# First scan: expert tiles handled in pairs, one tanh and two VectorE operations for both

## The reference, cut to what matters

```python
xn = layernorm(x)
# scan: h is kept for each of 256 features and 16 states
h = dA_t * h + dBx_t ;  y_t = einsum('bdn,bn->bd', h, C_t)
# experts: 176 inner rows
h = silu(x @ w_gate.T) * (x @ w_up.T) ;  acc = acc + h @ w_down.T * cw
x = x + scan(xn) + experts(xn)
```

## Time and profile before

| | |
|---|---|
| median of three runs | 1195.89 us (1195.59 to 1200.48) |
| profiled execution, its own time | 1205.48 us |
| its span, first to last instruction | 1203.7 us |
| busy TensorE, VectorE | 976.7, 914.1 us |
| busy ScalarE, GpSimd | 497.0, 434.9 us |
| mean granted TensorE clock | 0.935 |

### The profile page before, as it was taken

One profiled execution on the slowest core, in us unless ns is written; L12 is line 12 of the kernel. 1 busy time (PEld: TensorE's weight loads), 2 busy tenths in 40 slices (PEclk: granted clock), 3 DMA queues, 4 the chain that ended last, 5 costly groups with the idle time before them and its releaser, 6 DMA issues. The chain is left out here.

```text
span 1203.7 us, 18601 instructions
## 1 busy us (share of the span) xinstructions
PE 976.7 (81%) x6048; PEld 578.1 (48%) x6048; DVE 914.1 (76%) x1506; ACT 497.0 (41%) x1130; POOL 434.9 (36%) x332
## 2 busy tenths in 40 slices
PE   3987997788787778773787686889988988899885
PEld 2354555444444444441634353445555555456553
DVE  4659567989999999999657746677677767677676
ACT  2201135554555555543121124545455554554542
POOL 0000100777787877753171010322322232133310
PEclk9989999989999999995798798999998999999998
DMA  6960172787878878878650041443433343244524
GB/s 220 369 172 1 52 164 74 134 155 144 165 148 156 162 149 159 147 141 182 142 148 5 0 99 38 112 95 86 112 87 93 87 106 93 67 95 104 116 40 141
DMA packets 107092, 143.27 MB, mean 119 GB/s; under 512 B 30022, under 2 KB 97334, under 8 KB 102710
## 3 DMA queue, kind: packets, MB, share of 16 engines
q0 software_dynamic: 30368, 77.92, 33.5%
q1 hardware_dynamic: 76630, 64.14, 19.2%
HBM read 72.80 MB, written 39.46 MB: 93 GB/s over the span
## 5 line engine op out<-in xcount | busy, mean ns | idle before, releaser
L1501 POOL DMA_INDIRECT sum<-yo,to_i x48 | 78.0, 1624 | 317.1 <-ACT yo L1459 301.2
L1171 POOL DMA_INDIRECT xg<-xn_d,token_i x80 | 96.2, 1203 | 175.1 <-DVE to_i L460 93.4
L1164 POOL DMA_INDIRECT sum<-yo,to_i x80 | 140.3, 1754 | 46.8 <-DMA sum<-yo,to_i 23.7
L1011 PE MATMUL bank<-areaA,xgT 128*128 x320 | 120.6, 502 | 15.0 <-issue 9.9
L1028 PE MATMUL bank<-areaA,hidT 88*128 x320 | 91.7, 410 | 45.8 <-ACT hidT L1076 41.7
L2048 DVE TENSOR_TENSOR areaD<-areaD,gb 128x512 f32<-128x512 f32 x128 | 87.5, 688 | 53.0 <-ACT areaD L1995 49.2
L1028 PEld LDWEIGHTS bank<-areaA,hidT 88*128 88x128 f32 x320 | 55.6, 193 | 76.7 <-issue 72.1
L686 PE MATMUL bank<-xnT,areaB 128*128 128x512 f32 x192 | 86.8, 599 | 0.8 <-DVE y L716 0.8
L1846 PE MATMUL bank<-xnT,w_in 128*128 128x512 f32 x160 | 85.5, 661 | 2.2 <-ACT ecn L1751 1.5
L1011 PEld LDWEIGHTS bank<-areaA,xgT 128*128 128x128 f32 x320 | 56.8, 196 | 58.0 <-issue 41.5
L1491 POOL DMA_INDIRECT xg<-xn_d,token_i x48 | 53.9, 1123 | 82.6 <-DVE to_i L460 68.2
(11 more groups left out here) (342 smaller groups left out, 2141.6 us busy)
## 6 DMA issues: line engine op xcount, KB each, us to landing
y<-xnT POOLq DMA_DIRECT2D x21, 1024.0 KB
wst<-gu_f SPq DMA_DIRECT2D x96, 176.0 KB
y<-areaB POOLq DMA_DIRECT2D x11, 1024.0 KB
wst<-down_f SPq DMA_DIRECT2D x48, 176.0 KB
areaA<-in_gu SPq DMA_DIRECT2D x2, 2816.0 KB
gu_f<-in_gu POOLq DMA_DIRECT2D x1, 5632.0 KB, 17.0
sum<-yo SPq DMA_DIRECT2D x2, 2176.0 KB, 16.2
down_f<-in_down POOLq DMA_DIRECT2D x1, 2816.0 KB, 22.6
```

Source lines behind the costliest of these rows:

```text
L1011: last = nc.tensor.matmul(bank[:, GB + q % 2, 0:2 * FI], xgT[:, q % 2, k, :], wgu0_of(e, k), start=(k == 0), stop=(k == KD - 1))
L1164: nc.gpsimd.indirect_dma_start(sum0_d[q % 2], bass.IndirectOffsetOnAxis(ap=to_i[:, q:q + 1], axis=0), yo[:, q % 5, :], None, compute_op=AL ...
L1171: nc.gpsimd.indirect_dma_start(xg[:, q % 5, :], None, xn_d[0], bass.IndirectOffsetOnAxis(ap=token_i[:, q:q + 1], axis=0)).then_inc(s.gathe ...
L1501: nc.gpsimd.indirect_dma_start(sum1_d, bass.IndirectOffsetOnAxis(ap=to_i[:, q:q + 1], axis=0), yo[:, q % 4, :], None, compute_op=ALU.add). ...
```

## The change

Tiles go in pairs of six ticks. tile_at(t, ahead, at) gives the tile q = 2m + ahead whose step stands at place `at` of pair m's six ticks, which begin at tick 6m + 1. One tanh of 128 x 2 x 176 reads both banks when both gate products are there (gu_full at q + 2), and the two VectorE operations work on both tiles. On TensorE the order in pair m is: hidden transposes of 2m, x transposes of 2m+2, down of 2m, gate and up of 2m+2, x transposes of 2m+3, hidden transposes of 2m+1, gate and up of 2m+3, down of 2m+1. On ScalarE: hT_copy 2m, xT_copy 2m+2, y_copy 2m, xT_copy 2m+3, hT_copy 2m+1, the tanh of pair m+1, y_copy 2m+1, with the decays at their ticks as before. VectorE does pair m's operations at tick 6m + 1. Before the loop the first two tiles are transposed and multiplied. GpSimd's and SyncE's lists are unchanged.

```diff
+        UNIT, TILE, PAIR = 4, 3, 6
+        def tile_at(t, ahead, at):
+            m, step = divmod(t - 1, PAIR)
+            q = 2 * m + ahead
+            return q if step == at and 0 <= q < NT0 else None
 def hid_transposes(pe, q):
-            pe.wait_ge(s.hid_ready, q + 1)
+            pe.wait_ge(s.hid_ready, q // 2 + 1)
 def layer0_tensor(pe):
-            x_transposes(pe, 0)
-            gate_up(pe, 0)
-            x_transposes(pe, 1)
+            for q in range(2):
+                x_transposes(pe, q)
+                gate_up(pe, q)
...
+                for ahead, at in ((0, 0), (1, 3)):
+                    q = tile_at(t, ahead, at)
+                    if q is not None: hid_transposes(pe, q)
+                q = tile_at(t, 2, 0)
+                if q is not None: x_transposes(pe, q)
...
+                for ahead, at in ((2, 2), (3, 3)):
+                    q = tile_at(t, ahead, at)
+                    if q is not None: gate_up(pe, q)
+                q = tile_at(t, 3, 2)
+                if q is not None: x_transposes(pe, q)
+                for ahead, at in ((0, 1), (1, 4)):
+                    q = tile_at(t, ahead, at)
+                    if q is not None: down(pe, q)
 def gate_tanh(act, q):
-            act.wait_ge(s.gu_full, q + 1)
-            nc.scalar.activation(act_t[:, q % 2, :], bank[:, GB + q % 2, 0:FI], ACT.Tanh, scale=0.5)
+            act.wait_ge(s.gu_full, q + 2)
+            nc.scalar.activation(act_t[:, :, :], bank[:, GB:GB + 2, 0:FI], ACT.Tanh, scale=0.5)
 def layer0_scalar(act):
+            xT_copy(act, 1)
             gate_tanh(act, 0)
-            xT_copy(act, 1)
...
+                q = tile_at(t, 2, 4)
+                if q is not None: gate_tanh(act, q)
+                for ahead, at in ((0, 0), (1, 3)):
+                    q = tile_at(t, ahead, at)
+                    if q is not None: hT_copy(act, q)
+                for ahead, at in ((2, 0), (3, 2)):
+                    q = tile_at(t, ahead, at)
+                    if q is not None: xT_copy(act, q)
+                for ahead, at in ((0, 1), (1, 4)):
+                    q = tile_at(t, ahead, at)
+                    if q is not None: y_copy(act, q)
 def silu(v, q):
-            v.wait_ge(s.tanh_ready, q + 1)
+            v.wait_ge(s.tanh_ready, q // 2 + 1)
-            first = scalar_tensor_tensor(act_t[:, q % 2, :], act_t[:, q % 2, :], 1.0, bank[:, GB + q % 2, 0:FI], ...)
+            first = scalar_tensor_tensor(act_t[:, :, :], act_t[:, :, :], 1.0, bank[:, GB:GB + 2, 0:FI], ...)
-            scalar_tensor_tensor(hid[:, q % 2, :], act_t[:, q % 2, :], 0.5, bank[:, GB + q % 2, FI:2 * FI], ...)
+            scalar_tensor_tensor(hid[:, :, :], act_t[:, :, :], 0.5, bank[:, GB:GB + 2, FI:2 * FI], ...)
 def layer0_vector(v):
-                if t == 1:
-                    silu(v, 0)
-                if part == 2 and q + 1 < NT0:
-                    silu(v, q + 1)
+                q = tile_at(t, 0, 0)
+                if q is not None: silu(v, q)
```

More of the change, by code:

```diff
@@ L952, in phase0_vector @@
             v.wait_ge(vec.sem, vec.now)
-        UNIT, TILE = 4, 3
+        UNIT, TILE, PAIR = 4, 3, 6
         TICKS0 = UN * UNIT
-        assert TICKS0 >= TILE * (NT0 + 2)
+        assert NT0 % 2 == 0 and TICKS0 >= TILE * (NT0 + 2)
+        def tile_at(t, ahead, at):
+            m, step = divmod(t - 1, PAIR)
+            q = 2 * m + ahead
+            return q if step == at and 0 <= q < NT0 else None
         BROW, CROW, XB, HY, GB = 0, 2, 4, 5, 6
@@ L1032, in layer0_tensor @@
             pe.wait_ge(s.w_expert, 64)
-            x_transposes(pe, 0)
-            gate_up(pe, 0)
-            x_transposes(pe, 1)
+            for q in range(2):
+                x_transposes(pe, q)
+                gate_up(pe, q)
             for t in range(TICKS0):
-                q, part = divmod(t, TILE)
                 pair = (t + 1) // (2 * UNIT)
@@ L1040, in layer0_tensor @@
                     b_product(pe, pair)
[L1041 to L1044, removed]
+                for ahead, at in ((0, 0), (1, 3)):
+                    q = tile_at(t, ahead, at)
+                    if q is not None:
+                        hid_transposes(pe, q)
+                q = tile_at(t, 2, 0)
+                if q is not None:
+                    x_transposes(pe, q)
                 if t and t % (2 * UNIT) == 0:
                     c_product(pe, t // (2 * UNIT))
[L1047 to L1050, removed]
+                for ahead, at in ((2, 2), (3, 3)):
+                    q = tile_at(t, ahead, at)
+                    if q is not None:
+                        gate_up(pe, q)
+                q = tile_at(t, 3, 2)
+                if q is not None:
+                    x_transposes(pe, q)
+                for ahead, at in ((0, 1), (1, 4)):
+                    q = tile_at(t, ahead, at)
+                    if q is not None:
+                        down(pe, q)
         def decay(act, u):
@@ L1068, in gate_tanh @@
         def gate_tanh(act, q):
-            act.wait_ge(s.gu_full, q + 1)
-            nc.scalar.activation(act_t[:, q % 2, :], bank[:, GB + q % 2, 0:FI], ACT.Tanh, scale=0.5).then_inc(s.tanh_ready, 1)
+            act.wait_ge(s.gu_full, q + 2)
+            nc.scalar.activation(act_t[:, :, :], bank[:, GB:GB + 2, 0:FI], ACT.Tanh, scale=0.5).then_inc(s.tanh_ready, 1)
         def hT_copy(act, q):
@@ L1095, in layer0_scalar @@
             act.wait_ge(delta_ready, 4)
+            xT_copy(act, 1)
             gate_tanh(act, 0)
-            xT_copy(act, 1)
             for t in range(TICKS0):
[L1099 to L1107, removed]
+                q = tile_at(t, 2, 4)
+                if q is not None:
+                    gate_tanh(act, q)
+                for ahead, at in ((0, 0), (1, 3)):
+                    q = tile_at(t, ahead, at)
+                    if q is not None:
+                        hT_copy(act, q)
+                for ahead, at in ((2, 0), (3, 2)):
+                    q = tile_at(t, ahead, at)
+                    if q is not None:
+                        xT_copy(act, q)
+                for ahead, at in ((0, 1), (1, 4)):
+                    q = tile_at(t, ahead, at)
+                    if q is not None:
+                        y_copy(act, q)
                 if t % UNIT == 0 and t // UNIT + 1 < UN:
@@ L1111, in silu @@
         def silu(v, q):
-            v.wait_ge(s.tanh_ready, q + 1)
-            first = vec.done(nc.vector.scalar_tensor_tensor(act_t[:, q % 2, :], act_t[:, q % 2, :], 1.0, bank[:, GB + q % 2, 0:FI], ALU.add, ALU.mult))
+            v.wait_ge(s.tanh_ready, q // 2 + 1)
+            first = vec.done(nc.vector.scalar_tensor_tensor(act_t[:, :, :], act_t[:, :, :], 1.0, bank[:, GB:GB + 2, 0:FI], ALU.add, ALU.mult))
             v.wait_ge(vec.sem, first)
-            nc.vector.scalar_tensor_tensor(hid[:, q % 2, :], act_t[:, q % 2, :], 0.5, bank[:, GB + q % 2, FI:2 * FI],
+            nc.vector.scalar_tensor_tensor(hid[:, :, :], act_t[:, :, :], 0.5, bank[:, GB:GB + 2, FI:2 * FI],
                                            ALU.mult, ALU.mult).then_inc(s.hid_ready, 1)
@@ L1124, in layer0_vector @@
             for t in range(TICKS0):
-                if t == 1:
-                    silu(v, 0)
-                q, part = divmod(t, TILE)
-                if part == 2 and q + 1 < NT0:
-                    silu(v, q + 1)
+                q = tile_at(t, 0, 0)
+                if q is not None:
+                    silu(v, q)
                 u = t // UNIT
```

## The result

The changed kernel takes **1233.71 us**, the median of four runs (1231.38 to 1235.96); the kernel before took 1198.18 beside it (1195.59 to 1205.55). The ratio is **1.0255 [1.0215, 1.0295]**: slower, as forecast, but by about 30 us instead of 7.7 (the two medians lie 35.5 us apart; four executions of before that spread over 10 us don't settle which of the two it is). 1203.6 was predicted, and 1233.7 lies outside the range of 1185 to 1222.

What follows compares the result with a forecast made beforehand. VectorE, nearly full in the first scan stage, was taken to bound the kernel. Stage 346.9 + 20.1 + 4.6 + 3.0 = 374.6 us, 7.7 more than now, gave 1203.6 us; range 1185 to 1222.

Steps and rivals of the forecast that it cites:

- VectorE's own work: First scan with the experts beside it: 309.3 scan, 36.4 pair operations, 1.2 left over, 346.9 us without any wait.
- waits, odd pairs, at the tanh: VectorE before an odd pair's operations: the loop is not hidden, 1.06 us of waiting 19 times, 20.1 us.
- waits at product b: VectorE waiting for TensorE's product b: nothing in the sum; waiting for b or c was named as a sign against.
- start: First tanh also needs the second tile, so first operation at 207.79 instead of 205.44; 4.6 us of waiting.
- TensorE's clock: Eight stretches at the lower clock level, up to 1.7 us each where the loop bounds; between 0 and 7, taken as 3 us.
- the base: Median 1195.89 us of the kernel before, to which the difference worked out in the profiled stage was added.
- VectorE's relief: 352-wide operations cost 0.19 more, tanh 0.15; pair operations 36.4 us against 42.4, stage 20.0 less with no wait.
- The closed loop: Pair's operations through TensorE and ScalarE to next pair's operations: 8.05 us, against VectorE's own 9.38 (even) and 6.99 (odd).
- Products b and c of 0.6 us fall into TensorE's waits in most pairs: Products b and c on TensorE, queued behind the new waits, find room there; no time added.
- its longest case: Longest loads, loop 9.48 us, waiting 47; then every fourth pair, whose b waits for its scan, adds up to 1.0, ten times.
- Rival 3: TensorE, waiting once per pair, is granted 1.2 instead of 2.4 GHz for longer: 32 us on top, 1236; chance 0.08.
- The prediction's own signs: Wrong if odd pairs' waits are missing or under half a microsecond, clock under 0.9, or VectorE waits for products b and c.

Runs made afterwards that it cites:

- e4: Changed kernel plus matmuls nobody reads, two at step 0 of a pair and four at step 5; 1217.29 us, ratio 1.0088.
- after: The changed kernel itself, tiles in pairs, against the kernel before; 1233.71 us, ratio 1.0255.
- e6: Changed kernel with one register load per tile on TensorE instead of two, those of 2m+2 ahead of the waits, on ScalarE too; 1229.57 us, ratio 1.0235.
- e1: Changed kernel with product b a tick earlier, ahead of the second gate product, in pairs with m = 3 mod 4; 1228.69 us, ratio 1.0186.
- e9: e7 without the merging: tanh and VectorE's operations by tile again; 1194.51 us, ratio 0.9927 to before.
- e7: Changed kernel with b earlier, odd pairs' operations a tick earlier, filler products and register loads ahead; 1193.12 us, ratio 0.9894 to before.
- e3: Changed kernel with tanh, operations and their waits by tile again, TensorE's order kept; 1231.93 us, ratio 1.0205.
- e0: The kernel before, unchanged, profiled once more; 1206.02 us in one execution.

## Why the prediction was right or wrong, step by step

The stage was predicted at 374.6 us and measured at 394.5. e4, whose clock is full, gives the clock's share, 394.5 - 377.5 = 17.0 (net of what the added products cost), and the waits at full clock:

| term | predicted | measured |
|---|---|---|
| VectorE's own work | 346.9 | 347.4 (e4: 377.5 less 30.1 of waits) |
| waits, odd pairs, at the tanh | 20.1 for both kinds | 9.0, all with m = 1 mod 4 |
| waits at product b | 0 | 16.5, of which 16.3 with m = 3 mod 4 |
| start | 4.6 | 4.56 |
| TensorE's clock | 3.0 | 17.0 |
| sum | 374.6 | 394.5 |

Of the 19.9 between the two, 14.0 is the clock, 5.4 the waits, 0.5 VectorE's work. The time missed by 30.1 us; the 10 beyond the stage are mostly the base, 1195.89 where the profiled execution took 1205.48.

- **VectorE's relief: right.** The 352-wide operations take 0.519 and 0.521 us and the tanh 0.463, as the slope between two measured widths gave; the work adds up to within 0.5 us.
- **The closed loop: right** where nothing else interferes. The pairs with m = 1 mod 4 come 8.03 us apart on average in e4, 8.05 was worked out from the earlier trace rows. It is right by steps too: in e4's pair m = 1 they take 1.12, 1.34, 1.23, 1.28, 1.13 and 1.98 (second gate product to VectorE), against 1.14, 1.34, 1.27, 1.28, 1.04 and 1.98. The second is partly luck, since the added products fill it there; in after's pair m = 13, which no fall touches, the two steps with loads take 0.99 and 1.52, 2.51 together against 2.61. The even pairs hide the loop, as forecast. e6 shows that the late register loads are in it.
- **"Products b and c of 0.6 us fall into TensorE's waits in most pairs": wrong for one pair in four.** The step asked whether TensorE had time for b, and not who waits for it and when. In pairs with m = 3 mod 4 it stands behind the second gate product, and VectorE's L1160, ahead of the pair's operations, needs it. Those pairs wait 16.3 in all instead of the 9.5 that the loop gave them (9 x 1.06), 6.8 more. The prediction named this pair's b only in its longest case. e1 shows it: with b moved those pairs take some 7.6 instead of 8.9 where the clock is full.
- **The clock: the step that failed most.** The term of 3.0 took over the kernel before's eight stretches (seven, and the fall at the end of the tiles) and took those on even pairs for hidden. There were 17, and 15 of them lay on even pairs. The 1.3 us to spare there did not hide them: such a pair takes 9.9 to 10.2 us instead of 9.37 (10.8 with a fall of twice the length), and a pair m = 1 mod 4 behind it waits 1.4 to 1.5 at the tanh instead of 1.0.

  In after 9.4 us of the waits stand at even pairs, which with a full clock have none, 14.3 instead of 9.0 at m = 1 mod 4, 18.0 instead of 16.5 at b: 16 of the 17.0.

  Rival 3 was the mechanism, with 32 us on top for it; it is 14.0 on top, 17.0 in all. That its time of 1236 lies near the measured 1233.71 is chance: it has 12 us too many in the stage (406.6) and starts from a base that was 10 too low.

  Its case against itself, "the share of TensorE's work hardly changes", holds by the busy sum, but the sum deceives, since TensorE is busy for 94% of the low stretches: in those at the full level it is busy for 75% of the time against 77% before. Its case for itself, that the clock dropped while TensorE was busy, takes the effect for the state before it. Ahead of that fall, at 240.4, TensorE of the kernel before waited too:

```profile
233.74 1.12 PE L1028 MATMUL bank<-areaA,hidT 88*128 x4 [0.86 <-ACT hidT L1076]
235.24 1.45 PE L1011 MATMUL bank<-areaA,xgT 128*128 x4 [0.38 <-issue]
...
238.29 0.60 PE L981 MATMUL bank<-parts,pick 96*128 96x512 bf16 x2 [1.16 <-DVE xnT L1145]
```

That the idle time of TensorE brings the falls is shown by e4, which fills part of it. Whether by its amount, a little more now, or by how it lies, in several waits of each pair, no run separates.
- **The prediction's own signs.** It named waits for b and a clock under 0.9 as what would make it wrong. The first came; the second nearly, at 0.91, which shows that the mark was set too low: the nine hundredths from 0.91 to e4's 1.00 were worth 17 us here.

The Trainium skill, "TensorE: Matmul & The Clock Gate", section "A second HAM failure mode: psum-queue depth-cycling", tells of a kernel that cycles through PSUM banks, with short idle times between groups of matmuls, whose clock goes back and forth between the levels at a loss of throughput. This case's trace agrees, with 17 falls, and 17.0 us regained once the idle times were partly filled. The Trainium skill's "Perfetto Trace Analysis", section "Optimizing Scalar/DVE Operations", ties the gain of larger operations to a saturated engine. The runs agree: 4.6 us between e9 and e7, where VectorE is busy 95% of the stretch, and nothing between e3 and after, where it is busy some 85% (though e3's clock was lower, 0.88 against 0.91).

What stays open: what the filler itself costs (17.0 is net of it), whether a filler of another size or place would do better, what pairs are worth against a kernel before with the same edits, and, as e0 says, what makes some executions of the kernel before shorter.

## What to carry to other kernels

When one wait comes to stand for two tiles whose buffers used to alternate, write down the closed loop that arises and set it against the other engine's own work pair by pair; but then go through every instruction that stands in order behind the loop's waits, and ask for each who needs it and when, not only whether there is room. On TensorE don't trust the busy sum across a change of its clock: it was 78% both times, at 0.96 and 0.91 of the full clock, with 1066 and 986 matmuls; count instructions, or compare stretches at one level. The edits of this loop didn't add up, since time saved at one wait was lost at the next or to the clock, so try such edits together before one is dropped.

## What the hardware showed unexpectedly

Three waits of TensorE of 1.00, 0.87 and 0.77 us, with matmuls between them, stood ahead of a fall to 1.2 GHz, and the fall lasted 3.4 us. More work made the stage faster: with products that nobody reads TensorE was busy for 31 us more from 206 to 550, and the stage was 17.0 us shorter. Why the falls mostly come two pairs apart was not tried and stays open.
